# Weight quantisation of a feed-forward block, spread over the stages before it, in a two-layer perceiver kernel on Trainium2

## The reference

```
z  = layernorm(x);   q, k = phi(z Wq + bq), phi(z Wk + bk);  v = z Wv + bv;  phi(y) = elu(y) + 1
x  = x + (causal linear attention of q, k, v) Wo + bo
z  = layernorm(x)
W' = clip(round(W / s), -128, 127) * s,  s = max|W| over a row / 127   for w_gate, w_up (1408 x 512), w_down (512 x 1408)
z' = the same with one scale for the whole of z;  h = silu(z' w_gate'^T) * (z' w_up'^T);  h' like z'
x  = x + h' w_down'^T
```

## Time and profile before

| what | before |
|---|---|
| median of three runs | 2219.57 us |
| the profiled execution | 2217.67 us |
| its span, first to last instruction | 2215.9 us |
| instructions | 44115 |
| busy: PE | 1968.0 us (89%) |
| busy: DVE | 1617.4 us (73%) |
| busy: ACT | 1004.3 us (45%) |
| busy: POOL | 664.5 us (30%) |
| mean granted TensorE clock, of full speed | 0.94 |

### The profile page before, as it was taken

How to read it: one execution, slowest core, us unless ns; L and a number is a source line. 1 busy time by engine, 2 the same in 40 slices (tenths; PEclk the granted TensorE clock), 3 DMA queues, 4 the chain that set the end, 5 groups by cost and what they waited for, 6 DMA issues and landing times. The chain is left out here.

```text
span 2215.9 us, 44115 instructions
## 1 busy us (share of the span) xinstructions
PE 1968.0 (89%) x17800; PEld 1085.6 (49%) x17800; DVE 1617.4 (73%) x2826; ACT 1004.3 (45%) x1420; POOL 664.5 (30%) x690
## 2 busy tenths in 40 slices
PE   6799999999688375899999999999999999667898
PEld 3355555555345222455555555555555555433643
DVE  4689999999565774587777777777777776635676
ACT  2699899989310332233333333333333333200453
POOL 3344445444210450133333233333333332213000
PEclk9899999999699578999999999999999999988899
DMA  4332333232031301000000000000000000120300
GB/s 144 96 79 73 89 96 81 69 92 58 29 117 55 148 0 38 27 16 22 22 21 22 22 22 22 22 22 22 22 22 22 3 21 2 49 72 0 118 40 19
DMA packets 40138, 106.16 MB, mean 48 GB/s; under 512 B 19328, under 2 KB 21632, under 8 KB 33792
## 3 DMA queue, kind: packets, MB, share of 16 engines
q1 hardware_dynamic: 39936, 103.35, 15.2%
HBM read 75.42 MB, written 1.05 MB: 35 GB/s over the span
## 5 line engine op out<-in xcount | busy, mean ns | idle before, releaser
L1360 POOL TENSOR_SCALAR a1c_p_hi<-a1c_pf 128x512 f16<-128x512 f32 x272 | 201.3, 740 | 666.1 <-ACT a1c_pf L1416 623.7
L365 POOL TENSOR_SCALAR a0c_p_hi<-a0c_r 128x1024 f16<-128x1024 f32 x128 | 154.6, 1208 | 269.0 <-DVE a0c_r L465 266.1
L1385 ACT ACTIVATE a1c_k_hi<-PS 128x512 f16<-128x512 f32 x136 | 81.2, 597 | 326.9 <-PE PS L1222 326.9
L470 DVE TENSOR_TENSOR a0c_p_lo<-a0c_r,a0c_p_hi 128x1024 f16<-128x1024 f32 x128 | 201.3, 1573 | 0.9 <-POOL a0c_p_hi L365 0.9
L1565 DVE TENSOR_TENSOR a1c_p_lo<-a1c_pf,a1c_p_hi 128x512 f16<-128x512 f32 x272 | 197.9, 729 | 4.9 <-POOL a1c_p_hi L1360 4.9
L1392 ACT ACTIVATE a1c_v_hi<-PS 128x512 f16<-128x512 f32 x136 | 81.5, 599 | 259.0 <-PE PS L1232 206.2
L1416 ACT ACTIVATE a1c_pf<-PS,a_maskc 128x512 f32<-128x512 f32 x256 | 174.9, 685 | 48.6 <-PE PS L1727 39.1
L1508 DVE CUSTOM_DVE_ANT_0 a1c_junk<-PS,a1c_maskr 128x512 bf16<-128x512 f32 x256 | 175.9, 687 | 18.4
L465 DVE TENSOR_TENSOR a0c_r<-PS,a0c_r 128x1024 f32<-128x1024 f32 x128 | 155.3, 1213 | 34.2 <-ACT a0c_r L411 34.1
L1483 DVE SCALAR_TENSOR_TENSOR a1c_k_lo<-PS,a1c_k_hi 128x512 f16<-128x512 f32 x136 | 93.8, 690 | 106.8 <-ACT a1c_k_hi L1385 106.8
L1490 DVE SCALAR_TENSOR_TENSOR a1c_v_lo<-PS,a1c_v_hi 128x512 f16<-128x512 f32 x136 | 94.0, 691 | 86.9 <-ACT a1c_v_hi L1392 86.7
(11 more groups left out here) (359 smaller groups left out, 4773.0 us busy)
## 6 DMA issues: line engine op xcount, KB each, us to landing
a_cf<-in_ctxT SPq DMA_DIRECT2D x16, 1024.0 KB, 5.2
a0c_ks<-a0c_k_hi SPq DMA_DIRECT2D x128, 128.0 KB, 2.4
a1c_cf<-in_ctx SPq DMA_DIRECT2D x16, 1024.0 KB, 4.9
a0c_ks<-a0c_k_lo SPq DMA_DIRECT2D x64, 128.0 KB, 2.3
f_w<-in_w SPq DMA_DIRECT2D x4, 1024.0 KB, 8.7
f_w<-in_w SPq DMA_DIRECT2D x1, 4096.0 KB, 19.9
s1q_w<-in_L1a_wT SPq DMA_DIRECT2D x3, 1024.0 KB, 7.7
w_gate_raw<-in_w_gate SPq DMA_DIRECT2D x1, 2816.0 KB, 9.5
```

The lines of the kernel that those rows point to most:

```text
L365: nc.gpsimd.tensor_scalar(p_hi[:, u % 4, :], r[:, u % 4, :], 1.0, 0.0, ALU.mult, ALU.add)\
L470: nc.vector.tensor_tensor(p_lo[:, u % 4, :], r[:, u % 4, :], p_hi[:, u % 4, :], ALU.subtract)\
L1360: nc.gpsimd.tensor_scalar(p_hi[:, v % 4, :], pf[:, v % 2, :], 1.0, 0.0, ALU.mult, ALU.add)\
```

## The change

What each part of the diff does:

1. A class `QuantisedWeights` holds the buffers, the semaphores and the steps of `quantised_weights`, whose block is gone. `largest` and `inverse` run on DVE, `shift` (multiply and add the rounding constant) now on ACT, `whole` (the conversion to bf16) on POOL, `turn` (transposes) on PE, `keep` (copies out of PSUM) on ACT.
2. For w_gate: loaded in block one of the linear attention as before; its largest values are found by DVE in three pieces between the bias additions to v; `shift` and `whole` run in block two.
3. For w_up: loaded in block one, behind the matrix for v, which is itself loaded there once q is made (its buffer is the one of Wq) and no longer in `l0ln`. `largest` and `inverse` stand at the head of DVE's list in block two, ahead of the first mask; `shift` and `whole` follow those of w_gate.
4. For w_down: loaded in block two when w_up is in bf16; `largest` and `inverse` stand in `add_product` between the bias and the first product; `shift` and `whole` follow in the same block.
5. w_gate is transposed and copied during `f0ln`: five copies stand ahead of the square root on ACT, six behind it. w_up is transposed and copied at the head of the feed-forward block, w_down between the gate and up products and the down product, its last six copies between the `hq` instructions.
6. The clip factors and the next attention's two matrices are loaded in `f0ln`. DVE takes the largest of z ahead of the clip arithmetic.
7. The split of `L1x_wv` is shared: ACT scales it and makes the high half in eight instructions of 128x1024 between the first eight silus; POOL makes the difference right after the first split, ahead of the second reduction.
8. Several buffers share memory (`z`, `zt` and `y`; `hT` and the raw w_up; `ex` and `pos` and the next attention's halves), and one `clear_semaphores` between the linear attention and the feed-forward block is gone.

```diff
@@ -124,8 +124,12 @@
             @block.scalar
             def _(act):
+                if copies is not None:
+                    copies(act, 0)
                 act.wait_ge(var_done, 1)
                 nc.scalar.activation(std[:], veps[:], ACT.Sqrt).then_inc(std_done, 1)
+                if copies is not None:
+                    copies(act, 1)
                 if zT is not None:
                     for k in (0, 1):
                         act.wait_ge(turned, k + 1)
@@ -222,6 +238,8 @@
                 for b in range(B):
                     nc.vector.tensor_tensor(g.x[:, b, :], g.x[:, b, :], bias[:], ALU.add).then_inc(based, 1)
                 dve.wait_ge(based, B)
+                if largest is not None:
+                    largest(dve)
                 for b in range(B):
                     dve.wait_ge(product, b + 1)
                     nc.vector.tensor_tensor(g.x[:, b, :], g.PS[:, 4 + b, :], g.x[:, b, :], ALU.add)\
...
-            z, zT = s.sb("z", [P, B, D]), s.sb("zT", [P, KT, D])
-            w = s.sb("w", [P, 3, KT, D])
+            z, zT = q[:, 0, :, :], s.sb("zT", [P, KT, D])
+            w = s.sb("w", [P, 2, KT, D])
...
-                              weights(2, "L0a_wvT"), (bv[:], d["L0a_bv"].broadcast_to([P, D]), w_in[2])])
+                              (bv[:], d["L0a_bv"].broadcast_to([P, D]), w_in[2])])
             with nc.Block() as block:
                 @block.sync
                 def _(sp):
-                    load(sp, [(g.gate_raw[:], d["w_gate"], g.gate_in)])
+                    qw.load(sp, d, "w_gate")
+                    sp.wait_ge(product, KT)
+                    load(sp, [weights(2, "L0a_wvT")])
+                    qw.load(sp, d, "w_up")
...
-                            mm = nc.tensor.matmul(g.PS[:, b, :], zT[:, t, b * P:(b + 1) * P], w[:, 2, t, :],
+                            mm = nc.tensor.matmul(g.PS[:, b, :], zT[:, t, b * P:(b + 1) * P], w[:, 0, t, :],
...
+                        if b == 0:
+                            qw.largest(dve, "w_gate", 0, 4)
+                        if b == 1:
+                            qw.largest(dve, "w_gate", 4, 8)
+                        if b == 2:
+                            qw.largest(dve, "w_gate", 8, FT0)
+                            qw.inverse(dve, "w_gate")
...
+                    qw.load(sp, d, "w_down")
+                @block.scalar
+                def _(act):
+                    qw.shift(act, "w_gate")
+                    qw.shift(act, "w_up")
+                @block.gpsimd
+                def _(pool):
+                    qw.whole(pool, "w_gate")
+                    qw.whole(pool, "w_up")
 
                 @block.tensor
...
                                 .then_inc(a_done, 1)
+                    qw.largest(dve, "w_up", 0, FT0)
+                    qw.inverse(dve, "w_up")
                     dve.wait_ge(tri_in, 16)
...
+        def largest(dve):
+            qw.largest(dve, "w_down", 0, KT)
+            qw.inverse(dve, "w_down")
+        add_product(nc, g, "l0p", a, wo, bo, out_loaded, largest=largest,
+                    shifts=lambda act: qw.shift(act, "w_down"), wholes=lambda pool: qw.whole(pool, "w_down"))
...
+    def load(self, sp, d, name):
+
+        if name == "w_down":
+            sp.wait_ge(self.int_done, self.BEFORE["w_down"])
+        sp.dma_start(self.raw(name), d[name]).then_inc(self.loaded[name], 16)
+
+    def largest(self, dve, name, i0, i1):
+
+        dve.wait_ge(self.loaded[name], 16)
+        self.nc.vector.tensor_reduce(self.scale[name][:, i0:i1], self.tiled(self.raw(name), name)[:, i0:i1, :], AX.X,
+                                     ALU.max, apply_absolute_value=True).then_inc(self.max_done, i1 - i0)
+
+    def inverse(self, dve, name):
+
+        j, n = self.NAMES.index(name), self.TILES[name]
+        dve.wait_ge(self.max_done, self.BEFORE[name] + n)
+        self.nc.vector.tensor_scalar(self.scale[name][:], self.scale[name][:], 1.0 / 127.0, None, ALU.mult)\
+            .then_inc(self.scale_done, 1)
+        dve.wait_ge(self.scale_done, j + 1)
+        self.nc.vector.reciprocal(self.inv[:, j, 0:n], self.scale[name][:]).then_inc(self.inv_done, 1)
+
+    def shift(self, act, name):
+
+        j = self.NAMES.index(name)
+        w = self.tiled(self.raw(name), name)
+        act.wait_ge(self.round_set, 1)
+        act.wait_ge(self.inv_done, j + 1)
+        for i in range(self.TILES[name]):
+            self.nc.scalar.activation(w[:, i, :], w[:, i, :], ACT.Identity, bias=self.round[:, 0:1],
+                                      scale=self.inv[:, j, i:i + 1]).then_inc(self.shifted, 1)
+
+    def whole(self, pool, name):
+
+        w, o = self.tiled(self.raw(name), name), self.tiled(self.ints(name), name)
+        if name != "w_gate":
+            pool.wait_ge(self.int_done, FT0)
+        for i in range(self.TILES[name]):
+            pool.wait_ge(self.shifted, self.BEFORE[name] + i + 1)
+            self.nc.gpsimd.tensor_scalar(o[:, i, :], w[:, i, :], 1.0, -ROUND, ALU.mult, ALU.add)\
+                .then_inc(self.int_done, 1)
+
...
+        def gate_turns(pe):
+            for i in range(FT0):
+                if i >= 8:
+                    pe.wait_ge(qw.copied, i - 7)
+                qw.turn(g, pe, "w_gate", i, i % 8)
+
+        def gate_copies(act, part):
+            for i in (range(5), range(5, FT0))[part]:
+                qw.keep(g, act, "w_gate", i, i % 8)
+        layer_norm(nc, g, "f0ln", g.x, z, turns=gate_turns, copies=gate_copies,
+                   loads=[(clip[:, 0:1], d["clip_x"].broadcast_to([P, 1]), clip_in),
+                          (clip[:, 1:2], d["clip_down"].broadcast_to([P, 1]), clip_in)]
+                   + [(raw[:, i, :], d[n], raw_in[i]) for i, n in enumerate(("L1x_wk", "L1x_wv"))])
...
+        zt, y = z, z
+        hT, hq = qw.tiled(qw.second_raw[:], "w_up"), m.sb("hq", [P, FT0, D], BF16)
...
-                def next_weights(n):
...
+
+                pool.wait_ge(top_done, 1)
+                nc.gpsimd.partition_all_reduce(tops[:, 0:1], top[:, 0:1], P, reduced_max).then_inc(all_done, 1)
+                hi, lo = g.next_weights[0]
+                pool.wait_ge(diag_done, KT)
+                pool.wait_ge(raw_in[0], 16)
+                nc.gpsimd.tensor_scalar(raw[:, 0, :], raw[:, 0, :], W_SCALE, 0.0, ALU.mult, ALU.add).then_inc(scaled, 1)
+                pool.wait_ge(scaled, 1)
+                nc.gpsimd.tensor_scalar(hi[:], raw[:, 0, :], 1.0, 0.0, ALU.mult, ALU.add).then_inc(w_hi_done, 1)
+                pool.wait_ge(w_hi_done, 1)
+                nc.gpsimd.tensor_tensor(lo[:], raw[:, 0, :], hi[:], ALU.subtract).then_inc(w_lo_done, 1)
+                hi, lo = g.next_weights[1]
+                pool.wait_ge(wv_hi_done, 4)
+                nc.gpsimd.tensor_tensor(lo[:], raw[:, 1, :], hi[:], ALU.subtract).then_inc(w_lo_done, 1)
+                pool.wait_ge(top_done, 2)
+                nc.gpsimd.partition_all_reduce(tops[:, 1:2], top[:, 1:2], P, reduced_max).then_inc(all_done, 1)
 
             @block.scalar
             def _(act):
                 act.wait_ge(clip_in, 32)
                 nc.scalar.activation(cexp[:], clip[:], ACT.Exp, scale=-1.0).then_inc(clip_exp, 1)
+                for i in range(FT0):
+                    qw.keep(g, act, "w_up", i, 4 + i % 4)
                 for k in (0, 1):
                     act.wait_ge(turned, k + 1)
                     nc.scalar.copy(zqT[:, k, :], g.PS[:, k, 0:256].bitcast(BF16)).then_inc(copied_a, 1)
...
                         act.wait_ge(h_done, i - 1)
                     nc.scalar.activation(sil[:, i % 2, :], g.PS[:, i % 4, :], ACT.Silu, scale=sgx[:, i:i + 1])\
                         .then_inc(sil_done, 1)
+                    part = slice(i // 2 * 1024, i // 2 * 1024 + 1024)
+                    if i < 8 and i % 2 == 0:
+                        act.wait_ge(raw_in[1], 16)
+                        nc.scalar.activation(raw[:, 1, part], raw[:, 1, part], ACT.Copy, scale=W_SCALE)\
+                            .then_inc(wv_scaled, 1)
+                    elif i < 8:
+                        act.wait_ge(wv_scaled, i // 2 + 1)
+                        nc.scalar.copy(g.next_weights[1][0][:, part], raw[:, 1, part]).then_inc(wv_hi_done, 1)
+                for i in range(5):
+                    qw.keep(g, act, "w_down", i, i % 3)
                 for i in range(FT0):
+                    if i + 5 < FT0:
+                        qw.keep(g, act, "w_down", i + 5, (i + 5) % 3)
                     act.wait_ge(hc_done, i + 1)
                     nc.scalar.activation(hq[:, i, :], hT[:, i, :], ACT.Copy, bias=-ROUND).then_inc(hq_done, 1)
 
...
+                nc.vector.tensor_reduce(top[:, 0:1], z[:].rearrange("p b n -> p (b n)"), AX.X, ALU.max,
+                                        apply_absolute_value=True).then_inc(top_done, 1)
                 dve.wait_ge(clip_exp, 1)
                 one(nc.vector.tensor_scalar(c1[:], cexp[:], 1.0, None, ALU.add))
                 one(nc.vector.reciprocal(csig[:], c1[:]))
```

(32 more changed lines are left out.)

179 lines of the change are left out of this document (63 added, 116 removed).

## The result

The changed kernel takes 2203.13 us (median of four runs, 2199.08 to 2206.75) against 2219.13 for the kernel before in the same series: a ratio of 0.9935, 95% interval 0.9913 to 0.9956. It is faster, by 16 us and not by the 48 of the forecast, and lies outside the range given. The profiled execution took 2206.75 us (span 2204.6), so the profiled executions differ by 10.9 us, and 37.1 us of the sum's 48.0 are missing there.

What follows compares the result with a forecast made beforehand. PE was taken to bound block two, while the quantisation stretch ran no matrix product and kept DVE busy. Terms summed to -48.0 us: 2169.7 profiled, 2171.6 as plain median, rounded to 2171; range 2163 to 2178 for 8 in 10.

Steps and rivals of the forecast that it cites:

- The block that goes: Quantisation block between `z` and the feed-forward block: 49.3 us go, with its work paid where it went.
- w_gate's largest values, the load for v, `shift` and `whole`, w_down's load: Linear attention, blocks one and two: reductions, loads and ACT's 15.6 us beside POOL all hidden, costing nothing.
- w_up at the head of block two: DVE's reduction ahead of the first mask makes PE stand: cost 5.0 us, between 4.8 and 5.7.
- The clock: Block two: PE's clock falls in the gap, about 5 us at half speed, costing 2.4 us, between 0 and 3.7.
- The slower rival: Block two's gap: the clock falls and doesn't come back; 55 us more, 2226 us; chance 0.01.
- w_down in `add_product`: Reduction and inverse ahead of the first product addition: hidden by 0.4 us, cost 0, up to 1.5.
- The barrier, `f0ln`: Ahead of and in `f0ln`: 0.6 us of barrier go; copies ahead of the root make it 7.5 us, costing 2.1.
- Head of the feed-forward block: Scale of z ready to be computed 2.9 us after the block opens, not 6.7: 3.8 us go.
- POOL ahead of the second reduction: Feed-forward block: the reduction of h waits for POOL's second difference, costing 2.0 us.
- The tail: End of the feed-forward block: the last addition to x is no longer held by POOL's difference; 5.8 us go.
- The rule weighed: Gate products: transposes don't count as busy for the clock, so the gates start as cold as before, 2171 us.
- the warm rival: Feed-forward block: transposes keep PE warm at the gates and down product; 5.2 us less, 2166 us; chance 0.14.

Runs made afterwards that it cites:

- e1_filler: Changed kernel with five more f32 128x512 products on PE in block two, ahead of the first product with v: 2178.87 us, 0.9819 of before.
- e4_resident: Changed kernel with one more POOL partition reduction, of a constant, during `f0ln`: 2197.47 us, 0.9908 of before.
- e6_diff_after: Changed kernel with POOL's second difference moved behind the second reduction and DVE's quantisation of h: 2193.88 us, 0.9894 of before.

## Why the prediction was wrong, point by point

*What bounds the kernel.* Right, and used too little: PE bounds block two, so whatever PE's clock does there is paid in full.

*The block that goes.* Right. It is gone, and what came in its place is charged below.

*w_gate's largest values, the load for v, `shift` and `whole`, w_down's load.* Right, all hidden. The reductions took 2.27, 2.28 and 1.74 us; ACT's 22 `shift` 15.6 us; nothing waited for either.

*w_up at the head of block two.* The wait was sized well (first mask at 6.6 us, PE idle 4.56 us; with PE kept busy, in `e1_filler`, the block is 4.8 us longer than before, against 5.0). No run shows its "up to 0.3 of blocking by POOL" as such; what the trace has is a first tiny instruction of 0.39 us instead of 0.17.

*The clock.* This is the step that failed. "It came back at 789.2, 5.6 us after the first gate product ... So I expect a fall, and about 5 us at half speed": the fall came, the return didn't, within the block. The 5.6 and 4.9 us are times after *dense 128x512 products*, and block two's are mostly 128x33. The forecast's term for it, 2.4 us, measured 28.9 - 4.8 = 24.1 us, and both the extra products in the gap and the split reduction give it back. The slower rival named the very mechanism and dismissed it with that argument, at 0.01. Its full price was not reached, because `add_product`'s dense products did bring the clock back (0.91 in 730 to 732 us), as my reason against it says of dense products; it only doesn't hold for block two.

*w_down in `add_product`.* Its reduction is hidden in the sense meant: POOL's last tile ended at 741.9 and DVE's last addition at 742.7. The 1.2 us there come from the clock: before, it fell in the stage's first microsecond and rose again between 700 and 701 us, 3 to 4 us into the product with Wo; now it is at 0.50 from the start and rises between 730 and 731, about 5 us into that product.

*The barrier, `f0ln`.* The barrier left 0.61 us instead of 0.33, so half of the 0.6 came. The layer norm takes 7.4 us, with 7.5 forecast:

```profile
743.42 2.54 ACT L951 COPY qw_qg<-PS 128x512 bf16<-128x512 bf16 x5 [2.98 <-PE PS L941]
745.98 1.28 ACT L130 ACT_TABLE_LOAD   x1
...
747.39 3.00 ACT L951 COPY qw_qg<-PS 128x512 bf16<-128x512 bf16 x6
```

(Timeline of ACT, kernel after: five copies at 0.51, the table load, six more.)

*Head of the feed-forward block.* This is the second step that failed. "2.29, POOL's 0.4 and the hand-overs give 2.9" counts a reduction that starts at once. It was 9.0, since the reduction comes 8.33 us after POOL's instruction ahead of it, whatever DVE has ready. Before, that time lay beside the clip loads and the maximum, which ended at the same moment (773.23 + 2.29 = 775.52), and was put down to it. Timeline of POOL, kernel before:

```profile
769.38 0.20 POOL L935 MEMSET f_ones<- 128x128 f32 x1 [6.45 <-POOLq L823]
775.65 0.38 POOL L948 PARTITION_ALL_REDUCE f_tops<-f_top  x1 [6.07 <-DVE f_top L995]
```

In moving DVE's maximum earlier the change took away its cover; I asked of DVE's instructions what stood ahead of them, and not of POOL's. The Trainium skill, "GPSIMD Engine Reference", on instruction dispatch, gives about 6 us (5.95) for the first call to a freshly loaded kernel, without a visible instruction in the profile. The 6.08, 5.87 and 5.64 us here agree in size. That it is a code load no trace shows; what they show is that it is owed again after ordinary instructions (5.87 us) and not after another reduction (`e4_resident`).

*POOL ahead of the second reduction.* Right that it waits for the difference (792.05), with 2.0 us; the idle time behind the difference, 6.08 us, makes it 8.0. The order was the wrong one: behind the difference POOL has no wait left in which that time could pass, as `e6_diff_after` shows.

*The tail.* Right. All four additions to x take 0.69 us each; the one of 7.57 is gone. The last of them in DVE's timeline, kernel after:

```profile
818.96 0.69 DVE L1116 TENSOR_TENSOR g_x<-g_x,f_z 128x512 f32<-128x512 f32 x1
```

*The rule weighed, and the warm rival.* Neither came out. With nothing on PE but bf16 transposes the clock rose from 0.50 to 1.00 between 754 and 755 us. That is against my reading of the earlier trace rows and against the sentence of the Trainium skill that was weighed ("TensorE: Matmul & The Clock Gate", Part 4, on transposes), but it isn't a rule either: in the kernel before, 44 of them without a break from 762.98 to 767.85 us left the clock at 0.50. It fell again before 758, while PE stood still 5.79 us for the late reduction, and the gates began at half clock as before. The table by stretches of PE, kernel after:

```profile
752.00:754.00 2.00, 1.79 (x17) 0.50 0.97 418
754.00:755.00 1.00, 0.93 (x11) 0.88 1.03 442
755.00:756.00 1.00, 0.81 (x9) 1.00 0.84 360
756.00:758.00 2.00, 0.02 (x1) 0.91 0.02 8
```

*The chances.* Faster was right, with a third of the forecast's gain, since all that was missed stayed below what the removed block saves; the range was not. It was built from errors of a microsecond or two in each term, and two of its terms had no upper bound in the trace: how long a half clock lasts in work like block two's, and a reduction on POOL with nothing ahead of it to hide the 6 us.

## What to carry to other kernels

Before work is put ahead of the first instruction that another engine waits for, ask how long TensorE will stand still and what it runs next: block two's short products with a weight load each didn't win the clock back, so that two to four idle microseconds cost the rest of that stage at half speed, where the same work cut in pieces behind the first hand-overs cost nothing. An idle time marked "issue" ahead of a partition reduction is a cost that belongs to it, wherever it is moved; here it was free only while POOL would have waited anyway. A cost read off one stage (here a clock's return) need not hold for a stage with other work.

## What the runs showed of the hardware

- TensorE's clock stayed at 0.50 through 48 us in which the records have it busy without a break, in a mix of eight f32 instructions of 128x33, each with its weights, to two of 128x512; the same mix held 1.00 in the kernel before. Eight 128x512 products back to back brought it to 1.00 in under 3 us.
- 0.66 us of idle time ahead of that mix left the clock at 1.00, 2.27 us was followed by a fall that cost 22 us in all. In the kernel before, 1.05 us ahead of block two left it, and 1.99 us behind block two was followed by a fall.
- bf16 transposes alone were followed by a rise to 1.00 in the kernel after (754 to 755 us) and not in the kernel before (762.98 to 767.85 us). What makes the difference is open.
- A partition reduction on POOL had 5.64 to 6.23 us of idle time named "issue" ahead of it after ordinary POOL instructions; after another reduction it started 0.1 us behind the maximum that it waited for. The idle time runs out while POOL waits for a semaphore. With 4 MB of loads in flight it was 7.81 to 8.33 us in five kernels; for the early reductions, whose idle time began before the loads moved data, 6.80 and 6.07.
